# The q part of a 5x5 grouped convolution on TensorE: fp32 products replaced by three products of split fp32r operands

## Chip, cores and metric

One Trainium2 chip, one of its cores. The metric is the device time of one execution, in microseconds; lower is better. The median of three executions of the kernel before is 5199.48 us (5190.54 to 5200.01).

## The reference, cut to what matters

Two layers on 4 images of 512 channels, 64x64 pixels. The change lies in the first one, a multi-scale linear attention:

```python
q = h @ wq.T; k = h @ wk.T; v = h @ wv.T                       # 512x512 each
qkv = moveaxis(concatenate([q, k, v], -1), -1, 1)
dw = conv(qkv, dw_kernel, 5x5, 'SAME', one group per channel)
pw = conv(dw, pw_kernel, 1x1, groups of 8 channels)
qkv_all = concatenate([qkv, pw], axis=1)
f = qkv_all.reshape(B, -1, 3 * 8, N)
query, key_ = relu(f[:, :, :8]), relu(f[:, :, 8:16]); value = f[:, :, 16:]
scores = einsum('bhdn,bhen->bhde', value_and_ones, key_)
out = einsum('bhde,bhen->bhdn', scores, query)
out = out[:, :, :-1] / (out[:, :, -1:] + 1e-15)
y = batchnorm(conv1x1(out)) + x
```

The second layer (edge filters, GELU, a gate, a 1x1 convolution and a layer norm) is not touched.

## The kernel before

The first layer runs in 16 passes: 4 images by 4 sets of 16 groups of channels ("heads"). A pass has two stages.

The *plain* stage computes q, k and v of the pass in 8 chunks of 512 pixels. It already uses split operands: ScalarE rounds x into `x_hi` (type fp32r), VectorE and GpSimd compute `x_lo` = x - x_hi, and TensorE adds three products, `w_hi x_hi`, `w_lo x_hi` and `w_hi x_lo` (lines 356 to 358). The results go to DRAM as tiles of 4x4 pixels with a halo, and come back as `loaded`, one head at a time, four buffers deep. At the end of the stage `mask_scores` writes the sums of the keys into `score_d` (lines 589 and 591) and TensorE multiplies `relu_q` by it (`denominate`, line 398); VectorE then inverts the sums (`invert`, line 628).

The *convolution* stage runs over 16 heads h. The depthwise 5x5 and pointwise 1x1 kernels of a head are multiplied into one matrix per shift of the tile grid: GpSimd's `build` makes `toeplitz` with three multiplications of 128x512 (t = q, k, v; line 733), two buffers deep, and starts on head h when TensorE has ended head h-2. TensorE's `conv_head` does q first: 4 matrix products of 128x128 by 256 columns in fp32 (line 431), each of which shows as two records, then k and v: 2 x 8 products of 128 columns each (line 441), two records each, with data that ScalarE's `gather` has laid out as `columns`. ScalarE copies q and v out of PSUM, VectorE k (`ckey_t`, line 671).

Order on the engines of the convolution stage, which is the order in the code:

- ScalarE, head h: gather(h+1), q out of PSUM (line 545), v of head h out of PSUM (line 485, the helper `copy`).
- VectorE, head h: `ckey_t` of head h; for h = 4 to 11 `divide`, two multiplications of 128x256 that wait for a load of `inverse`; at h = 3 `mixed_weights`; at h = 7 `split_weights` for the next pass, a cast of 128x1536 to `w_hi` and a subtraction to `w_lo` (lines 605 and 607), in 15 of the 16 passes.
- GpSimd: `build` for heads 2 to 15. Those for heads 0 and 1 lie in the plain stage.
- SyncE issues all DMAs: the q results to DRAM, the load of a later head, and the writes and loads of `divide`.

Of the kernel before, what the change touches and what calls it, by code (L numbers as in the profile page):

```python
# [6 lines left out]
F32 = mybir.dt.float32  # L7
# [3 lines left out]
F32R = mybir.dt.float32r  # L11
# [4 lines left out]
P = 128  # L16
# [38 lines left out]
def attention(nc, banks, io, dram):  # L55

    with ExitStack() as ctx:
        def sb(name, shape):
            return ctx.enter_context(nc.sbuf_tensor(name, shape, F32))
# [21 lines left out]
        value_t = sb("value_t", [P, 2, 4, P + 1])  # L81
        ckey_t = sb("ckey_t", [P, HV * PL, P])
        cvalue_t = sb("cvalue_t", [P, HV * PL, P + 1])
        loaded = sb("loaded", [P, LR, 3, TN])
        columns = sb("columns", [P, 2, 2, HV + 1, TG * HT])
        toeplitz = sb("toeplitz", [P, 2, 3, len(SHIFTS) * M])
        q_stage = sb("q_stage", [M, 2, TT])
        score_n = sb("score_n", [P, P])
        score_d = sb("score_d", [P, NCH * P])
        score_t = sb("score_t", [P, P])  # L90
        w_proj = sb("w_proj_part", [P, C])
        scale_row = sb("scale_row", [P, C])
# [48 lines left out]
        columns_ready = sem("columns_ready")  # L141
        head_done = sem("head_done")
        toeplitz_ready = sem("toeplitz_ready")
        cready = [sem(f"conv_{n}_ready") for n in "qk"]
        cevac = [sem(f"conv_{n}_evacuated") for n in "qkv"]
        q_written = [sem(f"q_written{i}") for i in range(2)]
# [39 lines left out]
        with nc.Block() as block:  # L186
# [161 lines left out]
            def _(pe):  # L348
# [41 lines left out]
                def denominate(it, half):  # L390
                    pe.wait_ge(sums_placed, 2 * it + half + 1)
                    if half == 0:
                        pe.wait_ge(evac[T_Q], NCH * (it + 1))
                    else:
                        pe.wait_ge(conv_q_loaded, 16 * (it + 1))
                    pe.wait_ge(den_evac, START + 2 * it + half)
                    for j in range(NCH):
                        last = nc.tensor.matmul(DEN_BANK[:, :], score_d[:, j * P:(j + 1) * P], rows((relu_q, relu_c)[half], j),
                                                start=(j == 0), stop=(j == NCH - 1))
                    last.then_inc(summed, 1)  # L400

# [20 lines left out]
                def conv_head(it, h):  # L422
                    w = toeplitz[:, h % 2, :, :].rearrange("p t (d m) -> p t d m", m=M)
                    q_bank, k_bank, v_bank = (of[h % 2] for of in CONV_BANKS)
                    x_q = loaded[:, h % LR, T_Q, :].rearrange("p (a c) -> p a c", c=TG)
                    pe.wait_ge(tiles_loaded[h % LR], 16 * (SH // LR) * it + 16 * (h // LR) + 16)
                    pe.wait_ge(toeplitz_ready, SH * it + h + 1)
                    if h >= 2:
                        pe.wait_ge(cevac[T_Q], SH * it + h - 1)
                    for d, (a, b) in enumerate(SHIFTS):  # L430
                        last = nc.tensor.matmul(q_bank[0:M, 0:TT], w[:, T_Q, d, :], x_q[:, a:a + TO, b:b + TO],  # L431
                                                start=(d == 0), stop=(d == len(SHIFTS) - 1))
                    last.then_inc(cready[T_Q], 1)

                    pe.wait_ge(columns_ready, SH * it + h + 1)
                    for t, bank in ((T_K, k_bank), (T_V, v_bank)):
                        if h >= 2:
                            pe.wait_ge(cevac[t], SH * it + h - 1)
                        for v in range(HV):
                            for d, (a, b) in enumerate(SHIFTS):  # L440
                                last = nc.tensor.matmul(bank[:, v * M:(v + 1) * M],  # L441
                                                        columns[:, h % 2, t - T_K, v + b, a * HT:(a + TO) * HT],
                                                        w[:, t, d, :], start=(d == 0), stop=(d == len(SHIFTS) - 1))
                        last.then_inc(cready[T_K] if t == T_K else head_done, 1)
# [38 lines left out]
            def _(act):  # L483
# [28 lines left out]
                def plain(it, conv_of):  # L512
                    if conv_of is not None:
                        act.wait_ge(divided, START + at(conv_of, 1, 0))
                    for j in range(NCH):
                        if j >= 2:
                            value_by_position(it, j - 2)
                        if conv_of is not None:
                            if j == 2:
                                scores_to_mix(conv_of, 1)  # L520
                        query(it, j)
                        if j + 1 < NCH:
                            round_x(it, j + 1)
                        key(it, j)
                    value_by_position(it, NCH - 2)
                    value_by_position(it, NCH - 1)

                def gather(it, h):

# [6 lines left out]
                    last.then_inc(columns_ready, 1)  # L536

                def conv(it, last):
                    gather(it, 0)
                    for h in range(SH):  # L540
                        if h + 1 < SH:
                            gather(it, h + 1)
                        act.wait_ge(cready[T_Q], SH * it + h + 1)
                        act.wait_ge(q_written[h % 2], 16 * START + 16 * (SH // 2 * it + h // 2))
                        nc.scalar.activation(q_stage[:, h % 2, :], CONV_BANKS[T_Q][h % 2][0:M, 0:TT], ACT.Relu).then_inc(cevac[T_Q], 1)
                        if h == 1:
                            scores_to_mix(it, 0)
                        if not last and h == SH - 2:
                            round_x(it + 1, 0)
                        act.wait_ge(head_done, SH * it + h + 1)  # L550
                        to = cvalue_t[:, :, h * HD:(h + 1) * HD].rearrange("p (s r) o -> p s r o", s=HV)
                        copy(to, CONV_BANKS[T_V][h % 2][:, 0:HV * M].rearrange("p (s o r) -> p s r o", o=HD, r=PL)).then_inc(cevac[T_V], 1)
# [19 lines left out]
            def _(dve):  # L572
# [6 lines left out]
                def mask_scores(it, half):  # L579

                    if half:
                        dve.wait_ge(scores_ready, it + 1)
                    else:
                        dve.wait_ge(chunk_scored, NCH * (it + 1))
                    nc.vector.tensor_copy(key_sum[:, :], SCORE_BANK[:, P:P + 1]).then_inc(key_sum_ready, 1)
                    dve.wait_ge(key_sum_ready, 2 * it + half + 1)
                    dve.wait_ge(den_evac, START + 2 * it + half)
                    apart, last = P + SH, (NCH - 1) * (P + SH)
                    nc.vector.tensor_scalar(score_d[:, 0:last].rearrange("p (j s) -> p j s", s=apart)[:, :, 0:SH],
                                            mask[:, None, :].to_broadcast([P, NCH - 1, SH]), key_sum[:, 0:1], None, ALU.mult)  # L590
                    nc.vector.tensor_scalar(score_d[:, last:last + SH], mask[:, :], key_sum[:, 0:1], None,
                                            ALU.mult).then_inc(sums_placed, 1)
                    dve.wait_ge(score_turned, 2 * it + half)
                    nc.vector.tensor_tensor(score_n[:, :].rearrange("p (h d) -> p h d", d=HD),
                                            SCORE_BANK[:, 0:P].rearrange("p (h d) -> p h d", d=HD),
                                            mask[:, :, None].to_broadcast([P, SH, HD]), ALU.mult).then_inc(scores_masked, 1)
# [44 lines left out]
                def mixed_weights(it, half):  # L641
                    dve.wait_ge(bn_inverted, 2)
                    dve.wait_ge(w_mixed, 2 * it + half + 1)
                    nc.vector.tensor_tensor(w_proj[:, :], W_BANKS[half][:, :], scale_row[:, :], ALU.mult).then_inc(w_out_ready, 1)

                def plain(it, conv_of):
                    for j in range(NCH):
                        if j == 4 and conv_of is not None:
# [10 lines left out]
                            split_x(it, j + 1)  # L659
                        value(it, j)  # L660
                        compress(it, j)
                    keys_by_position(it, NCH - 2)
                    keys_by_position(it, NCH - 1)
                    mask_scores(it, 0)
                    invert(it, 0)

                def conv(it, more):
                    for h in range(SH):
                        dve.wait_ge(cready[T_K], SH * it + h + 1)
                        to = ckey_t[:, :, h * HD:(h + 1) * HD].rearrange("p (s r) o -> p s r o", s=HV)  # L670
                        nc.vector.tensor_scalar(  # L671
# [45 lines left out]
            def _(pool):  # L717
# [5 lines left out]
                def build(it, h):  # L723
# [4 lines left out]
                    for t in range(3):  # L728
# [3 lines left out]
                        point = g[:, NTAP:GT][:, None, :, None].to_broadcast([P, len(SHIFTS), HD, PL])  # L732
                        last = nc.gpsimd.tensor_tensor(  # L733
                            toeplitz[:, h % 2, t, :].rearrange("p (d o r) -> p d o r", o=HD, r=PL), tap, point, ALU.mult)
                    last.then_inc(toeplitz_ready, 1)

                def plain(it):
# [695 lines left out]
```

## Time and profile before

| | |
|---|---|
| median of three executions | 5199.48 us |
| the profiled execution | 5196.7 us |
| its span, first to last instruction | 5194.8 us |
| mean clock of TensorE granted, as a share of full speed | 0.976 |
| TensorE, matrix products busy | 4887.5 us, 94% |
| VectorE busy | 2583.4 us, 50% |
| ScalarE busy | 2021.1 us, 39% |
| GpSimd busy | 1223.1 us, 24% |
| lines 356 to 358, the split products of the plain stage | 1536 each, 610.9, 599.7 and 601.2 us |
| line 431, q of the convolution | 2048 records, 485.9 us |
| line 441, k and v of the convolution | 8192 records, 955.7 us |

PE is TensorE, PEld its loads of weights, DVE VectorE, ACT ScalarE, POOL GpSimd. Records of TensorE overlap, as matrix products are pipelined: the distance from one start to the next tells what one costs, not its duration. The first layer takes up the first 3114 us or so of the span, the second layer the rest.

### The profile page before, as it was taken

The page shows a single profiled execution, that of the slowest core. Times are in us where ns is not written, and L with a number is a line of the kernel's source. Part 1 is how long each engine was busy: PE and PEld are TensorE (multiplying, and loading weights), DVE is VectorE, ACT ScalarE, POOL GpSimd, SP SyncE. Part 2 cuts the span into 40 slices and gives each one's busy share as a digit, 9 for nine tenths or more (in the row PEclk, how much of TensorE's full clock was granted, in tenths as well). Part 3 has the DMA queues.
Part 4 walks back from the last instruction along what each step waited for, and adds up shares of the span by engine and source line. Part 5 has one row for each costly group of instructions (what it writes and reads, how often), then busy time and mean ns, then how long its engine had stood idle before and what let it go on. Part 6 is the DMA issues. An engine that isn't in the chain of part 4 may idle for free. (4 is left out here: it accounts for less than half of the span.)

```text
span 5194.8 us, 65292 instructions
## 1 busy us (share of the span) xinstructions
PE 4887.5 (94%) x22760; PEld 3445.3 (66%) x22760; DVE 2583.4 (50%) x3635; ACT 2021.1 (39%) x3671; POOL 1223.1 (24%) x1030
## 2 busy tenths in 40 slices
PE   8999999999999999999999996899899989998958
PEld 7887887888888888888888883344344434443423
DVE  3333333333334334424434421786688578847865
ACT  3333333333333333333323320454555455545555
POOL 2342342342342332332332330000300020011003
PEclk9999999999999999999999998999999999999969
DMA  6666665666666666666656644443344344434313
GB/s 188 198 208 202 197 214 199 198 212 205 198 216 202 204 206 206 206 197 215 206 186 225 203 151 168 142 155 112 130 136 150 108 144 130 141 118 135 117 35 115
DMA packets 390811, 893.09 MB, mean 172 GB/s; under 512 B 33488, under 2 KB 66512, under 8 KB 388240
## 3 DMA queue, kind: packets, MB, share of 16 engines
q1 hardware_dynamic: 390544, 889.18, 51.8%
q8 instruction: 211, 3.46, 0.3%
q14 instruction: 56, 0.46, 0.0%
HBM read 588.74 MB, written 300.32 MB: 171 GB/s over the span
## 5 line engine op out<-in xcount | busy, mean ns | idle before, releaser
L733 POOL TENSOR_TENSOR toeplitz<-taps 128x512 f32<-128x512 f32 x768 | 889.1, 1185 | 955.2 <-PE bank L441 955.2
L441 PEld LDWEIGHTS bank<-toeplitz,columns 128*128 128x128 f32 x8192 | 954.4, 192 | 13.9
L441 PE MATMUL bank<-toeplitz,columns 128*128 128x128 f32 x8192 | 955.7, 275 | 0.0
L1029 PE MATMUL bank<-att,w_proj 128*128 128x512 f32 x2048 | 909.6, 598 | 34.1 <-DVE centred L1314 23.8
L1029 PEld LDWEIGHTS bank<-att,w_proj 128*128 128x128 f32 x2048 | 393.0, 192 | 531.8 <-issue 523.3
L356 PE MATMUL bank<-x_hi,w_hi 128*128 128x512 f32 x1536 | 610.9, 398 | 18.4 <-DVE x_lo L600 18.4
L1362 POOL TENSOR_TENSOR centred<-centred,x_out 128x512 f32<-128x512 f32 x128 | 164.5, 1318 | 1937.1 <-ACT centred L1176 1937.1
L358 PE MATMUL bank<-x_lo,w_hi 128*128 128x512 f32 x1536 | 601.2, 391 | 0.0
L357 PE MATMUL bank<-x_hi,w_lo 128*128 128x512 f32 x1536 | 599.7, 390 | 0.0
L1042 PE MATMUL bank<-edge,w_branch 128*128 128x512 f32 x1024 | 494.5, 629 | 96.1 <-ACT edge L1130 96.1
L671 DVE TENSOR_SCALAR ckey_t<-bank 128x256 f32<-128x256 f32 x256 | 107.4, 419 | 881.8 <-PE bank L441 881.4
L431 PE MATMUL bank<-loaded,toeplitz 128*128 128x256 f32 x2048 | 485.9, 379 | 3.4 <-POOL toeplitz L733 3.4
L1064 PE MATMUL bank<-feat,w_image 128*128 128x512 f32 x1024 | 453.4, 601 | 10.3 <-DVE w_image L1330 10.3
L600 DVE TENSOR_TENSOR x_lo<-x_sb,x_hi 128x1536 fp32r<-128x1536 f32 x128 | 251.7, 1966 | 421.9 <-ACT x_hi L485 421.9
L1042 PEld LDWEIGHTS bank<-edge,w_branch 128*128 128x128 f32 x1024 | 204.1, 202 | 370.8 <-issue 283.4
L720 POOL TENSOR_TENSOR x_lo<-x_sb,x_hi 128x512 fp32r<-128x512 f32 x128 | 165.6, 1293 | 1074.5 <-ACT x_hi L485 1074.5
L431 PEld LDWEIGHTS bank<-loaded,toeplitz 128*128 128x128 f32 x2048 | 370.5, 190 | 62.0 <-issue 15.5
L485 ACT ACTIVATE cvalue_t<-bank 128x256 f32<-128x256 f32 x256 | 102.6, 401 | 773.7 <-PE bank L441 773.7
L1064 PEld LDWEIGHTS bank<-feat,w_image 128*128 128x128 f32 x1024 | 197.0, 193 | 259.2 <-issue 249.8
L356 PEld LDWEIGHTS bank<-x_hi,w_hi 128*128 128x128 f32 x1536 | 289.6, 189 | 76.3 <-DMA mask<-in_head_mask 12.6
L358 PEld LDWEIGHTS bank<-x_lo,w_hi 128*128 128x128 f32 x1536 | 289.4, 188 | 62.3
L357 PEld LDWEIGHTS bank<-x_hi,w_lo 128*128 128x128 f32 x1536 | 289.9, 189 | 57.6
(115 smaller groups left out, 5629.8 us busy)
## 6 DMA issues: line engine op xcount, KB each, us to landing
x_sb<-in_x_tiled SPq DMA_DIRECT2D x128, 1024.0 KB, 6.4
tiles_dram<-tiles SPq DMA_DIRECT2D x128, 867.0 KB, 6.8
loaded<-tiles_dram SPq DMA_DIRECT2D x256, 433.5 KB, 4.0
inverse<-inverse_dram SPq DMA_DIRECT2D x256, 256.0 KB, 5.0
att_dram<-out_sb SPq DMA_DIRECT2D x256, 256.0 KB, 4.1
att<-att_dram SPq DMA_DIRECT2D x64, 1024.0 KB, 6.3
xb<-x_dram SPq DMA_DIRECT2D x128, 330.0 KB, 3.2
x_out<-in_x_pad SPq DMA_DIRECT2D x32, 1056.0 KB, 5.5
```

Of the source, the lines that this page charges most:

```text
L356: nc.tensor.matmul(banks[t][:, :], wh, xh, start=(k == 0), stop=False)
L357: nc.tensor.matmul(banks[t][:, :], wl, xh, start=False, stop=False)
L358: last = nc.tensor.matmul(banks[t][:, :], wh, xl, start=False, stop=(k == KT - 1))
L431: last = nc.tensor.matmul(q_bank[0:M, 0:TT], w[:, T_Q, d, :], x_q[:, a:a + TO, b:b + TO], start=(d == 0), stop=(d == len(SHIFTS) - 1))
L441: last = nc.tensor.matmul(bank[:, v * M:(v + 1) * M], columns[:, h % 2, t - T_K, v + b, a * HT:(a + TO) * HT], w[:, t, d, :], start=(d == ...
L600: nc.vector.tensor_tensor(x_lo[:, j % XR, X_DVE, :], x_sb[:, j % XR, X_DVE, :], x_hi[:, j % XR, X_DVE, :].bitcast(F32), ALU.subtract).then ...
L720: nc.gpsimd.tensor_tensor(x_lo[:, j % XR, X_POOL, :], x_sb[:, j % XR, X_POOL, :], x_hi[:, j % XR, X_POOL, :].bitcast(F32), ALU.subtract).t ...
L733: last = nc.gpsimd.tensor_tensor(toeplitz[:, h % 2, t, :].rearrange("p (d o r) -> p d o r", o=HD, r=PL), tap, point, ALU.mult)
L1029: last = nc.tensor.matmul(P_BANKS[m][:, :], w_proj[:, i * HALF + k, m * P:(m + 1) * P], att[:, i, k, :], start=(i == 0 and k == 0), stop=( ...
L1042: last = nc.tensor.matmul(banks[e][:, :], w_branch[:, k, e, :], edge[:, k % 2, e, :], start=(k == 0), stop=(k == KT - 1))
L1064: last = nc.tensor.matmul(Z_BANKS[n % len(Z_BANKS)][:, :], w_image[:, k, m * P:(m + 1) * P], feat[:, k, j * CH:(j + 1) * CH], start=(k == ...
L1362: nc.gpsimd.tensor_tensor(y, y, x_out[:, j % 2, m, :].rearrange("p (r w) -> p r w", w=W2)[:, :, 1:W + 1], ALU.add).then_inc(out_ready, 1)
```

## The change

The q part of the convolution takes split operands too.

- ScalarE rounds q's tiles of a head into `q_hi` (`round_q`, 128x289) and q's matrices into `tq_hi` (`round_taps`, 128x512). Both have one buffer. In head h it does this for head h+1, right after q has been copied out of PSUM, ahead of the copy of v.
- VectorE subtracts: `split_q` (128x289) and `split_taps` (128x512), for head h+1, at the top of head h, ahead of `ckey_t`. The differences `q_lo` and `tq_lo` take the places of `loaded` and `toeplitz` in memory.
- TensorE does 12 products of 256 columns in fp32r in place of 4 in fp32. They wait for `q_split` and `tq_split`; the wait for all three matrices of a head moves behind q.
- For head 0, `round_taps` lies in the plain stage on ScalarE at j = 5, `split_taps` on VectorE at j = 6, `round_q` at the head of the convolution stage and `split_q` between `mask_scores` and `invert`.
- `score_d` shrinks from 1024 to 240 columns. One write of 128x16 takes the place of writes of 128x112 and 128x16, and TensorE reads it at 8 offsets.

```diff
@@ -81,12 +81,18 @@
...
         cvalue_t = sb("cvalue_t", [P, HV * PL, P + 1])
-        loaded = sb("loaded", [P, LR, 3, TN])
+        with nc.sbuf_tensor("loaded", [P, LR, 3, TN], F32) as loaded:
+            pass
+        q_lo = ctx.enter_context(nc.sbuf_tensor("q_lo", [P, LR, 3, TN], F32R))
         columns = sb("columns", [P, 2, 2, HV + 1, TG * HT])
-        toeplitz = sb("toeplitz", [P, 2, 3, len(SHIFTS) * M])
+        with nc.sbuf_tensor("toeplitz", [P, 2, 3, len(SHIFTS) * M], F32) as toeplitz:
+            pass
+        tq_lo = ctx.enter_context(nc.sbuf_tensor("tq_lo", [P, 2, 3, len(SHIFTS) * M], F32R))
+        tq_hi = ctx.enter_context(nc.sbuf_tensor("tq_hi", [P, len(SHIFTS) * M], F32R))
+        q_hi = ctx.enter_context(nc.sbuf_tensor("q_hi", [P, TN], F32R))
         q_stage = sb("q_stage", [M, 2, TT])
         score_n = sb("score_n", [P, P])
-        score_d = sb("score_d", [P, NCH * P])
+        score_d = sb("score_d", [P, 2 * P - SH])
         score_t = sb("score_t", [P, P])
@@ -395,7 +406,7 @@
...
                     for j in range(NCH):
-                        last = nc.tensor.matmul(DEN_BANK[:, :], score_d[:, j * P:(j + 1) * P], rows((relu_q, relu_c)[half], j),
+                        last = nc.tensor.matmul(DEN_BANK[:, :], score_d[:, P - SH * (j + 1):2 * P - SH * (j + 1)], rows((relu_q, relu_c)[half], j),
                                                 start=(j == 0), stop=(j == NCH - 1))
@@ -422,16 +433,22 @@
...
                     q_bank, k_bank, v_bank = (of[h % 2] for of in CONV_BANKS)
-                    x_q = loaded[:, h % LR, T_Q, :].rearrange("p (a c) -> p a c", c=TG)
-                    pe.wait_ge(tiles_loaded[h % LR], 16 * (SH // LR) * it + 16 * (h // LR) + 16)
-                    pe.wait_ge(toeplitz_ready, SH * it + h + 1)
+                    wide = tq_hi[:, :].rearrange("p (d m) -> p d m", m=M)
+                    x_hi_q = q_hi[:, :].rearrange("p (a c) -> p a c", c=TG)
+                    x_lo_q = q_lo[:, h % LR, T_Q, :].rearrange("p (a c) -> p a c", c=TG)
+                    pe.wait_ge(q_split, SH * it + h + 1)
+                    pe.wait_ge(tq_split, SH * it + h + 1)
                     if h >= 2:
...
                     for d, (a, b) in enumerate(SHIFTS):
-                        last = nc.tensor.matmul(q_bank[0:M, 0:TT], w[:, T_Q, d, :], x_q[:, a:a + TO, b:b + TO],
-                                                start=(d == 0), stop=(d == len(SHIFTS) - 1))
+                        high, low = x_hi_q[:, a:a + TO, b:b + TO], x_lo_q[:, a:a + TO, b:b + TO]
+                        narrow = tq_lo[:, h % 2, T_Q, d * M:(d + 1) * M]
+                        nc.tensor.matmul(q_bank[0:M, 0:TT], wide[:, d, :], high, start=(d == 0), stop=False)
+                        nc.tensor.matmul(q_bank[0:M, 0:TT], narrow, high, start=False, stop=False)
+                        last = nc.tensor.matmul(q_bank[0:M, 0:TT], wide[:, d, :], low, start=False, stop=(d == len(SHIFTS) - 1))
                     last.then_inc(cready[T_Q], 1)
+                    pe.wait_ge(toeplitz_ready, SH * it + h + 1)
                     pe.wait_ge(columns_ready, SH * it + h + 1)
@@ -521,9 +538,19 @@
...
                             round_x(it, j + 1)
+                        if j == 5:
+                            round_taps(it, 0)
                         key(it, j)
...
                     value_by_position(it, NCH - 1)
+
+                def round_q(it, h):
+                    act.wait_ge(tiles_loaded[h % LR], 16 * (SH // LR) * it + 16 * (h // LR) + 16)
+                    copy(q_hi[:, :], loaded[:, h % LR, T_Q, :]).then_inc(q_rounded, 1)
+
+                def round_taps(it, h):
+                    act.wait_ge(tq_built, SH * it + h + 1)
+                    copy(tq_hi[:, :], toeplitz[:, h % 2, T_Q, :]).then_inc(tq_rounded, 1)
@@ -536,6 +563,7 @@
...
                 def conv(it, last):
+                    round_q(it, 0)
                     gather(it, 0)
@@ -543,6 +571,9 @@
...
                         nc.scalar.activation(q_stage[:, h % 2, :], CONV_BANKS[T_Q][h % 2][0:M, 0:TT], ACT.Relu).then_inc(cevac[T_Q], 1)
+                        if h + 1 < SH:
+                            round_q(it, h + 1)
+                            round_taps(it, h + 1)
                         if h == 1:
@@ -585,10 +616,7 @@
...
                     dve.wait_ge(den_evac, START + 2 * it + half)
-                    apart, last = P + SH, (NCH - 1) * (P + SH)
-                    nc.vector.tensor_scalar(score_d[:, 0:last].rearrange("p (j s) -> p j s", s=apart)[:, :, 0:SH],
-                                            mask[:, None, :].to_broadcast([P, NCH - 1, SH]), key_sum[:, 0:1], None, ALU.mult)
-                    nc.vector.tensor_scalar(score_d[:, last:last + SH], mask[:, :], key_sum[:, 0:1], None,
+                    nc.vector.tensor_scalar(score_d[:, P - SH:P], mask[:, :], key_sum[:, 0:1], None,
                                             ALU.mult).then_inc(sums_placed, 1)
@@ -642,6 +670,14 @@
...
                     nc.vector.tensor_tensor(w_proj[:, :], W_BANKS[half][:, :], scale_row[:, :], ALU.mult).then_inc(w_out_ready, 1)
+
+                def split_q(it, h):
+                    dve.wait_ge(q_rounded, SH * it + h + 1)
+                    nc.vector.tensor_tensor(q_lo[:, h % LR, T_Q, :], loaded[:, h % LR, T_Q, :], q_hi[:, :].bitcast(F32), ALU.subtract).then_inc(q_split, 1)
+
+                def split_taps(it, h):
+                    dve.wait_ge(tq_rounded, SH * it + h + 1)
+                    nc.vector.tensor_tensor(tq_lo[:, h % 2, T_Q, :], toeplitz[:, h % 2, T_Q, :], tq_hi[:, :].bitcast(F32), ALU.subtract).then_inc(tq_split, 1)
@@ -659,13 +695,19 @@
...
                         compress(it, j)
+                        if j == 6:
+                            split_taps(it, 0)
                     keys_by_position(it, NCH - 2)
...
                     mask_scores(it, 0)
+                    split_q(it, 0)
                     invert(it, 0)
...
                     for h in range(SH):
+                        if h + 1 < SH:
+                            split_q(it, h + 1)
+                            split_taps(it, h + 1)
                         dve.wait_ge(cready[T_K], SH * it + h + 1)
@@ -732,6 +774,8 @@
...
                             toeplitz[:, h % 2, t, :].rearrange("p (d o r) -> p d o r", o=HD, r=PL), tap, point, ALU.mult)
+                        if t == T_Q:
+                            last.then_inc(tq_built, 1)
                     last.then_inc(toeplitz_ready, 1)
```

Left out of the diff are the five new semaphores.

## Rows read from the trace of the kernel before

**Rows 1.** The page: busy time of TensorE, its busy tenths and clock
```profile
PE 4887.5 (94%) x22760; PEld 3445.3 (66%) x22760; DVE 2583.4 (50%) x3635; ACT 2021.1 (39%) x3671; POOL 1223.1 (24%) x1030
...
PE   8999999999999999999999996899899989998958
...
PEclk9999999999999999999999998999999999999969
```

**Rows 2.** One convolution stage: busy PE, PEld, DVE, ACT, POOL, then clock
```profile
1467.00:1555.00 88.00, 87.33 (x654) 82.98 (x653) 29.04 (x38) 29.40 (x77) 47.30 (x43) 1.00 0.63 200
```

**Rows 3.** Waits of TensorE, 300 to 3100 us: us in total, times, longest
```profile
PE bank L398 <- DVE score_d L591: 13.7, 14, 1.0
...
PE bank L431 <- POOL toeplitz L733: 3.2, 9, 0.5
```

**Rows 4.** Timeline, head 7 of one pass: start, duration, engine, operation
```profile
1505.43 1.90 PE L431 MATMUL bank<-loaded,toeplitz 128*128 128x256 f32 x8
...
1505.67 3.34 POOL L733 TENSOR_TENSOR toeplitz<-taps 128x512 f32<-128x512 f32 x3 [2.22 <-PE bank L441]
1505.91 1.17 ACT L485 ACTIVATE columns<-loaded 128x272 f32<-128x272 f32 x3
...
1507.16 3.73 PE L441 MATMUL bank<-toeplitz,columns 128*128 128x128 f32 x32
1507.36 0.38 ACT L545 ACTIVATE q_stage<-bank 128x256 f32<-128x256 f32 x1 [0.27 <-PE bank L431]
...
1509.34 0.41 DVE L671 TENSOR_SCALAR ckey_t<-bank 128x256 f32<-128x256 f32 x1
...
1510.73 1.89 PE L431 MATMUL bank<-loaded,toeplitz 128*128 128x256 f32 x8
```

**Rows 5.** The same timeline, VectorE and GpSimd in heads 8 and 9
```profile
1510.96 1.90 DVE L637 TENSOR_TENSOR out_sb<-relu_q,inverse 128x256 f32<-128x256 f32 x2 [1.22 <-DMA inverse<-inverse_dram]
1510.97 4.39 POOL L733 TENSOR_TENSOR toeplitz<-taps 128x512 f32<-128x512 f32 x3 [1.97 <-PE bank L441]
...
1512.70 1.76 DVE L605 CAST w_hi<-w_sb 128x1536 fp32r<-128x1536 f32 x1
...
1514.49 2.49 DVE L607 TENSOR_TENSOR w_lo<-w_sb,w_hi 128x1536 fp32r<-128x1536 f32 x1
...
1516.28 4.17 POOL L733 TENSOR_TENSOR toeplitz<-taps 128x512 f32<-128x512 f32 x3 [0.91 <-PE bank L441]
```

**Rows 6.** Timeline of TensorE, split products of 512 columns in the plain stage
```profile
1587.07 0.39 PE L357 MATMUL bank<-x_hi,w_lo 128*128 128x512 f32 x1
1587.30 0.39 PE L358 MATMUL bank<-x_lo,w_hi 128*128 128x512 f32 x1
```

**Rows 7.** Instructions by source line, 300 to 3100 us: duration ns min/median/max
```profile
L600 DVE TENSOR_TENSOR x_lo<-x_sb,x_hi x112: 1748/1759/2604, 390.2 to 2982.7; 128x1536 fp32r<-128x1536 f32 x112
...
L605 DVE CAST w_hi<-w_sb x14: 946/1762/1773, 350.8 to 2860.9; 128x1536 fp32r<-128x1536 f32 x14
...
L485 ACT ACTIVATE x_hi<-x_sb x224: 621/1050/1487, 383.1 to 2981.2; 128x512 fp32r<-128x512 f32 x112
```

**Rows 8.** Timeline, end of a plain stage and first head
```profile
1459.73 0.28 DVE L589 TENSOR_SCALAR score_d<-mask,key_sum 128x112 f32<-128x112 f32 x1
1459.93 0.22 DVE L591 TENSOR_SCALAR score_d<-mask,key_sum 128x16 f32<-128x16 f32 x1
...
1468.38 3.35 DVE L628 RECIPROCAL den_sb<-den_sb 128x512 f32<-128x512 f32 x1
```

**Rows 9.** A wait of TensorE, then three stretches (columns of Rows 2)
```profile
4955.88 7.62 PE L1042 MATMUL bank<-edge,w_branch 128*128 128x512 f32 x11 [4.02 <-ACT edge L1130]
...
4946.00:4951.00 5.00, 4.53 (x7) 1.98 (x8) 4.45 (x7) 2.60 (x5) 0.00 (x0) 0.66 0.26 68
...
4955.00:4961.00 6.00, 5.12 (x6) 2.19 (x7) 5.83 (x10) 4.14 (x7) 0.00 (x0) 0.50 0.21 56
...
1454.00:1462.00 8.00, 4.81 (x28) 3.63 (x29) 2.82 (x8) 3.10 (x8) 0.00 (x0) 1.00 0.80 289
```

More of the change, by code:

```diff
@@ L143, in attention @@
         toeplitz_ready = sem("toeplitz_ready")
+        tq_built = sem("toeplitz_q_built")
+        tq_rounded = sem("toeplitz_q_rounded")
+        tq_split = sem("toeplitz_q_split")
+        q_rounded = sem("q_tiles_rounded")
+        q_split = sem("q_tiles_split")
         cready = [sem(f"conv_{n}_ready") for n in "qk"]
```

## The prediction

> **What bounds the kernel now.** I read the page first. TensorE is busy 94% of the span, and in the first 24 of the 40 slices, the first layer, its digit is 9 after one 8, and so is the clock's in nearly all [rows 1]. Next, the busy time of one convolution stage: 87.33 of 88 us on TensorE, every other engine at most 54% [rows 2]. Then what TensorE waits for between 300 and 3100 us: in the convolution stage only 3.2 us, for GpSimd's matrices [rows 3]. So in this stage time is made of TensorE's cadence, and last the timeline gives that cadence. In head 7, q starts at 1505.43, k and v at 1507.16, the next q at 1510.73 [rows 4]. Head: 5.30 us; q 1.73, k and v 3.57. Shorten q and the head gets shorter, as long as what feeds q is ready in time. That is what the change puts at stake: q now waits for a chain over two engines with single buffers.
>
> **The products.** Removed per head: 1.73 us. Added: 12 products of 256 columns in fp32r. No row shows that width. From above: split products of 512 columns start 0.227 us apart [rows 6], where two fp32 streams of 256 columns, with their loads, take 1.73/8 = 0.217. If the extra 0.010 to 0.014 us is a fixed cost of each fp32r product, one of 256 columns costs 0.107 + 0.014 = 0.121. From below: line 441 loads a 128x128 matrix for every record and starts one each 3.57/32 = 0.112 us; nothing in the stage does better. I take the middle, 0.117, so 12 x 0.117 = 1.40 us, 0.33 less per head, 256 x 0.33 = **84 us saved** (with 0.112: 100; with 0.121: 72). The head becomes 4.97 us.
>
> The Trainium skill (TensorE: Matmul & The Clock Gate, Back-to-back issue gap) gives 262 cycles for 256 columns, 0.109 us; by that the sum would save 24 us more than mine. It states this without naming fp32r, and the fp32r rows at 512 columns lie above its rule (518 cycles, 0.216 us), so the row decides.
>
> **The chain for the next q, in a usual head.** Count from q's start in head h. ScalarE gathers head h+1 until 1.65 (1507.08 - 1505.43) [rows 4]. q's last product ends near 1.6. Then q out of PSUM, 0.38; `round_q` of 289 columns, about 0.45 (gather's 272 take 1.17/3 = 0.39 each); `round_taps` of 512, 0.63 (the 621 ns minimum) [rows 4, 7]. Adjacent ones overlap by 0.1, so `q_hi` is there at 2.4 and `tq_hi` at 3.0. VectorE subtracts: line 600 takes 1.75 for 1536 columns with two SBUF inputs [rows 7], so 1.04 ns a column plus 0.15: 0.45 for `split_q`, 0.68 for `split_taps`. GpSimd builds until 0.24 + 3.08 = 3.3, and holds VectorE up: see below. `split_q` 3.3 to 3.6, `split_taps` to 4.3. q of h+1 may start at 4.3; TensorE is free at 4.97. The chain hides with 0.7 us to spare, and k and v of head h are its cover. Without it, q would wait in each of 256 heads. `ckey_t`, now behind the splits, ends near 4.6 instead of 4.3; k's bank is wanted two heads later. v's copy waits for v anyway. ScalarE's load, 0.3+1.17+0.38+1.1 = 3.0 of 4.97, fits.
>
> **The turns at the port.** The rows show that VectorE's subtractions and multiplications with two SBUF inputs, and its cast, don't run beside GpSimd's multiplications; one waits for the other. Line 605 takes 0.946 at least and 1.76 in the middle [rows 7]; here 1.76, while three builds take 4.39 us in place of 3.08 (line 600 alone shows that 2.49 for `w_lo` is 0.74 too much) [rows 5, 7]. They take strict turns, since each engine's next instruction asks after its last has let go. Per turn: a build 0.95, a half of `divide` 0.35, `w_hi` 0.85, `w_lo` 1.65, and from these widths `split_q` 0.35, `split_taps` 0.65.
>
> In heads 4 to 11 `divide` delays the builds by up to two turns, 0.7 us, and so the splits. At worst I get the last split at 4.9 after q's start: still under 4.97.
>
> **Heads 7 to 9, where it doesn't fit.** `split_weights` stands in head 7 of VectorE, ahead of the splits for head 9. Count from q's start in head 8. `divide` starts near 0.05, behind the splits for head 8. Turns: half 0.35, build 0.95, half 0.35, build 0.95, `w_hi` 0.85, build 0.95, `w_lo` 1.65: over at 6.1. (Before, it ended at 1516.98 - 1510.73 = 6.25 in this pass [rows 4, 5], harmless, since TensorE needed nothing from it.) Meanwhile head 8 has ended at 4.97, and GpSimd asks for its turn with the build for head 10. So: build 0.95, `split_q` 0.35, build 0.95, `split_taps` 0.65 and 0.1 to be seen: q of head 9 starts at 9.1 to 9.2 and not at 4.97. **4.2 us lost in each of 15 passes, 63 us.** Late next is only `ckey_t` of head 8, behind the splits, and `divide`, whose loads of `inverse` SyncE sends; splits for head 10 find GpSimd done. Bounds: 2.3 us if GpSimd gets no turn in between (34 us), 4.6 with a late `inverse` (69).
>
> **What that wait does to the clock.** In the last stage TensorE waits 4.02 us for `edge` again and again; right after, the clock stands at 0.50 for a stretch with 5.12 us of work, and at 0.66 in one of 5 us after another such wait [rows 9]: that is 1.2 in place of 2.4 GHz, 2.6 and 1.7 us lost. A stretch at the end of a plain stage with 3.2 idle us of 8, in pieces, leaves it at 1.00 [rows 9]. TensorE would idle about 4 us here, after and before dense work. I take 2.0 us per pass, **30 us**; bounds 0 and 2.6 x 15 = 39.
>
> **The rest.** In head 0 the inversion (3.35 us from 1468.38) [rows 8] ends 4.4 after q's start; the splits for head 1 follow it and end at 5.3, TensorE is free at 4.97 + 0.11: 0.2 x 16 = 3 us lost. The smaller `score_d` takes 0.20 us off (line 591 starts that much after 589) [rows 8], and TensorE waits for it [rows 3]: 16 x 0.2 = 3 us saved. The waits for GpSimd at q, 3.2 us by the record and some 5 with what the modelled ends hide [rows 3], go: the wait for the whole build is behind q now. `round_taps` and `split_taps` of the plain stage, 0.6 and 0.7 us once a pass, lie beside chunks of about 10 us of products; below that cover, they would cost 21 us. The steps for head 0 at the head of the convolution stage lie under `denominate`, 7 us. SyncE's order and the number of DMAs don't change.
>
> **Sum.** -84 - 5 - 3 + 3 + 63 + 30 = +4 us. The profiled execution took 5196.7 (span 5194.8 and 1.9 around it), 2.8 below the median; on the median, 5199.5 + 4 = 5203.
>
> **Rivals.** (1) The turns and the wait are as above, but the clock stays up: no row shows a lone wait of 4 us in dense work of this stage. Sum -26: 5173. Against it: each wait of 4.02 us in the last stage looks alike. (2) GpSimd gets no turn between the splits; TensorE idles 2.3 us, and the clock loses 10 us at most: -84 - 5 + 34 + 10 = -45, 5154. Against it: the turns in rows 5. (3) Slower by more: the chain doesn't fit in the usual head. It decides from 0.7 us: with a longer semaphore path or one more build turn between `split_q` and `split_taps`, the last split lands at 5.2 to 5.3, 0.3 x 240 = 72 us more: 5275. For it: `build` is already pushed back in 8 of the heads. (4) fp32r products of 256 columns read from rows of 16 don't stream at one column per cycle. At the fp32 rate of 0.217 x 2 each, 12 take 5.2 us, 3.5 more than before: 5199 + 890 = 6090. Against it: 512 columns run at 0.227. (5) The products take 0.112, all else as forecast: 5188.
>
> **How the numbers follow.** A measurement of this kernel can tell about 0.2%, 10 us, from no change. My forecast, 5190 to 5232 with the bounds of product and clock: 0.45; of that, faster 0.05, same 0.25, slower 0.15. Rival 1: 0.18, rival 2: 0.12, rival 5: 0.10, all nearly faster. Rival 3: 0.11, rival 4: 0.04, slower. Together faster 0.42, same 0.28, slower 0.30. The range 5145 to 5240 leaves out rivals 4, most of 3, and a little at the lower end. Forecast's own range: 5180 to 5230.
>
> **What would show it.** In the timeline after: q's first record to k's first, 1.34 to 1.45 us. Usual heads 4.9 to 5.0 apart. TensorE's wait for VectorE's `tq_lo` ahead of head 9 near 4 us, 15 times, and none over 0.3 elsewhere; around it the turns build, `split_q`, build, `split_taps`. A dip of the clock's digits between slices 1 and 24. Wrong, if heads 2 to 7 are longer than 5.1, if `split_taps` follows `split_q` at once behind `w_lo`, or if the clock stays up.

## The result

The changed kernel takes 5218.09 us (median of 6 runs, 5216.56 to 5224.15), the kernel before 5197.91 (median of 6): the ratio is 1.0043, 95% interval 1.0031 to 1.0056, so 0.43% slower, some 20 us. The forecast was 5203, within 5145 to 5240, and gave slower a chance of 0.30. The profiled execution is the slowest of the six, 5224.15 us, with a span of 5222.3. The medians and ratios of the experiments leave out two executions at a lower granted clock: 13090.41 us (0.507) of the second experiment and 5833.38 us (0.835) of the fourth.

The page after: TensorE's busy share is 93%, its tenths look as before [rows 1], and so do the clock's. I had expected a dip in the clock's digits, and there is none: a slice is 130 us long, and a wait of 4 us in it, with the slow microseconds behind it, doesn't change a digit. The mean over the whole span shows it, 0.969 against 0.976.

```profile
PE 4858.9 (93%) x23784; PEld 3468.8 (66%) x23784; DVE 2946.3 (56%) x4115; ACT 2236.4 (43%) x4183; POOL 1222.0 (23%) x1030
...
PE   8999999999999999999999996899899989998958
...
PEclk9999999999999999999999998999999999999969
```

The waits of TensorE between 300 and 3100 us, which is where it shows (us in total, times, longest): 15 waits, 3.5 us each, ahead of q's first product. "issue" means that the record names no releaser. The waits for GpSimd's matrices at q [rows 3] are gone, and the one for `score_d` is 2.6 us shorter.

```profile
PE bank L446 <- issue: 52.8, 15, 3.9
...
PE bank L409 <- DVE score_d L619: 11.1, 14, 0.8
```

A usual head after, the timeline of head 6 in the same pass as [rows 4]. Read it as a chain. q's products start every 0.125 us (eleven steps from 1511.89 to k's first at 1513.27; the stamp of the group's first product is early by some 0.1 us, and behind products of 512 columns, which end head 1, by 0.4). q leaves PSUM at 1513.56, `q_hi` and `tq_hi` follow, `split_q` waits for the last build (1.13 us in place of 0.45), `split_taps` ends at 1516.04, and TensorE starts the next q at 1516.76, right behind v: 5.08 us after the last.

```profile
1511.68 0.37 PE L446 MATMUL bank<-q_hi,tq_hi 128*128 128x256 f32 x1
...
1511.89 0.29 PE L447 MATMUL bank<-q_hi,tq_lo 128*128 128x256 f32 x1
...
1512.01 3.10 POOL L775 TENSOR_TENSOR toeplitz<-taps 128x512 f32<-128x512 f32 x3 [1.97 <-PE bank L458]
...
1513.14 0.29 PE L448 MATMUL bank<-q_lo,tq_hi 128*128 128x256 f32 x1
...
1513.27 3.73 PE L458 MATMUL bank<-toeplitz,columns 128*128 128x128 f32 x32
1513.56 0.38 ACT L573 ACTIVATE q_stage<-bank 128x256 f32<-128x256 f32 x1
1513.84 0.44 ACT L502 ACTIVATE q_hi<-loaded 128x289 fp32r<-128x289 f32 x1
...
1514.17 0.62 ACT L502 ACTIVATE tq_hi<-toeplitz 128x512 fp32r<-128x512 f32 x1
1514.31 1.13 DVE L676 TENSOR_TENSOR q_lo<-loaded,q_hi 128x289 fp32r<-128x289 f32 x1 [2.01 <-ACT q_hi L502]
...
1515.36 0.68 DVE L680 TENSOR_TENSOR tq_lo<-toeplitz,tq_hi 128x512 fp32r<-128x512 f32 x1
...
1515.96 0.41 DVE L713 TENSOR_SCALAR ckey_t<-bank 128x256 f32<-128x256 f32 x1
...
1516.76 0.37 PE L446 MATMUL bank<-q_hi,tq_hi 128*128 128x256 f32 x1
```

Heads 8 and 9, the answer to [rows 5]. `w_lo` ends at 1528.38, 6.3 us after q's start. Then the turns: a build, `split_q` until 1529.61, a build, `split_taps` until 1531.06. q of head 9 starts at 1531.17 after an idle 3.74 us; the head took 9.05 us.

```profile
1522.12 0.36 PE L446 MATMUL bank<-q_hi,tq_hi 128*128 128x256 f32 x1
1522.16 3.61 POOL L775 TENSOR_TENSOR toeplitz<-taps 128x512 f32<-128x512 f32 x3 [1.99 <-PE bank L458]
...
1522.62 2.37 DVE L665 TENSOR_TENSOR out_sb<-relu_q,inverse 128x256 f32<-128x256 f32 x2 [0.27 <-DMA inverse<-inverse_dram]
...
1523.69 3.74 PE L458 MATMUL bank<-toeplitz,columns 128*128 128x128 f32 x32
...
1524.83 1.76 DVE L633 CAST w_hi<-w_sb 128x1536 fp32r<-128x1536 f32 x1
...
1526.62 1.76 DVE L635 TENSOR_TENSOR w_lo<-w_sb,w_hi 128x1536 fp32r<-128x1536 f32 x1
...
1527.51 4.47 POOL L775 TENSOR_TENSOR toeplitz<-taps 128x512 f32<-128x512 f32 x3 [1.74 <-PE bank L458]
...
1528.30 1.31 DVE L676 TENSOR_TENSOR q_lo<-loaded,q_hi 128x289 fp32r<-128x289 f32 x1
1529.53 1.53 DVE L680 TENSOR_TENSOR tq_lo<-toeplitz,tq_hi 128x512 fp32r<-128x512 f32 x1
...
1531.17 0.55 PE L446 MATMUL bank<-q_hi,tq_hi 128*128 128x256 f32 x1 [3.74 <-issue]
```

The clock over the same microseconds (columns of [rows 2], the clock is third from the end): 1.00 before the wait, 0.50 right after it.

```profile
1522.00:1527.00 5.00, 4.96 (x43) 4.91 (x43) 4.69 (x6) 2.69 (x7) 3.61 (x3) 1.00 0.68 216
1527.00:1531.00 4.00, 0.43 (x4) 0.24 (x3) 4.00 (x4) 1.44 (x4) 3.49 (x3) 1.00 1.00 323
1531.00:1534.00 3.00, 2.83 (x13) 2.87 (x14) 1.95 (x4) 0.00 (x0) 0.98 (x1) 0.50 0.11 40
```

### The profile page after: what moved, and what is told of

Its sections match the earlier page's. It is cut to its first block and busy times, and to the rows that moved or that the text cites. A ratio compares the mean times of both kernels' runs of the same rounds, so it can differ in the third digit from the quotient of the medians.

```text
span 5222.3 us, 68364 instructions
## 1 busy us (share of the span) xinstructions
PE 4858.9 (93%) x23784; PEld 3468.8 (66%) x23784; DVE 2946.3 (56%) x4115; ACT 2236.4 (43%) x4183; POOL 1222.0 (23%) x1030
## 5 line engine op out<-in xcount | busy, mean ns | idle before, releaser
L458 PE MATMUL bank<-toeplitz,columns 128*128 128x128 f32 x8192 | 967.5, 277 | 0.0
L676 DVE TENSOR_TENSOR q_lo<-loaded,q_hi 128x289 fp32r<-128x289 f32 x256 | 236.0, 922 | 490.7 <-ACT q_hi L502 490.6
L446 PE MATMUL bank<-q_hi,tq_hi 128*128 128x256 f32 x1024 | 332.0, 324 | 58.0 <-issue 56.4
L448 PE MATMUL bank<-q_lo,tq_hi 128*128 128x256 f32 x1024 | 301.4, 294 | 0.0
```

The lines of the kernel that those rows point to most:

```text
L446: nc.tensor.matmul(q_bank[0:M, 0:TT], wide[:, d, :], high, start=(d == 0), stop=False)
L448: last = nc.tensor.matmul(q_bank[0:M, 0:TT], wide[:, d, :], low, start=False, stop=(d == len(SHIFTS) - 1))
L458: last = nc.tensor.matmul(bank[:, v * M:(v + 1) * M], columns[:, h % 2, t - T_K, v + b, a * HT:(a + TO) * HT], w[:, t, d, :], start=(d == ...
L676: nc.vector.tensor_tensor(q_lo[:, h % LR, T_Q, :], loaded[:, h % LR, T_Q, :], q_hi[:, :].bitcast(F32), ALU.subtract).then_inc(q_split, 1)
```

## The experiments

Each was run beside the kernel before on the same chip, the first four on one chip, the others on a second: its ratio is to the kernel before there. The median spacing of the heads comes from the starts of q's first products in each trace, over the 16 passes.

**The weights' split in heads 12 and 13.** Is VectorE's backlog at `split_weights` the cause?

```diff
-                        if more and h == 7:
+                        if more and h == 12:
+                            round_weights(it + 1)
+                        if more and h == 13:
                             split_weights(it + 1)
```

(`round_weights` is the cast with its load's wait, `split_weights` the subtraction.)

> The changed kernel, with the cast to w_hi moved from head 7 to head 12 of VectorE and the subtraction to w_lo to head 13, where divide is over. Theory (backlog on VectorE): the wait of 3.74 us ahead of head 9's q goes, heads 8 and 9 take 5.07 us like the others in place of 9.0 and 6.4 to 7.6, and no half-clock stretch is left in the convolution stage. That is 15 x (3.95 + 1.3 or more) = 80 us less: about 5138 us. Rival (VectorE has too little room in any head, so the wait only moves): the same wait ahead of head 14 or 15, within 15 us of the changed kernel's 5218.

5137.79 us, ratio 0.9889 (0.9874 to 0.9904). Head 8 has a median of 5.07 us, head 9 of 5.06; head 14 takes 5.20. In its timeline `w_lo` of head 13 runs until 1131.57 and pushes the build to 1134.73, the build pushes both splits, and `split_taps` ends at 1135.28, 0.1 us before q starts. That is 0.13 us in each of 15 passes, 2 us. The long wait is gone and next to nothing came back for it: the rival falls. One wait is left in the profiled run, in head 7 of one pass. The timeline shows whose it is: `divide` waited 4.97 us for its load of `inverse` and kept the splits behind it on VectorE. Behind this wait too the clock is down, 0.64 over the 4 us from 1483. So a late load can do what the weights did, but once in 16 passes, not in 15.

```profile
1476.09 3.74 PE L458 MATMUL bank<-toeplitz,columns 128*128 128x128 f32 x32
...
1479.09 1.09 DVE L667 TENSOR_TENSOR out_sb<-relu_q,inverse 128x256 f32<-128x256 f32 x2 [4.97 <-DMA inverse<-inverse_dram]
...
1482.84 0.36 PE L446 MATMUL bank<-q_hi,tq_hi 128*128 128x256 f32 x1 [3.01 <-issue]
```

**Work inside the wait.** Is head 9 long because of the clock?

```diff
+                    if h == 9:
+                        pe.wait_ge(den_evac, START + 2 * it + 1)
+                        for j in range(4):
+                            nc.tensor.matmul(DEN_BANK[:, :], ident[:, :], rows(relu_q, j), start=True, stop=True)
                     pe.wait_ge(q_split, SH * it + h + 1)
```

> The changed kernel; in head 9, ahead of the wait for the splits, TensorE does 4 extra fp32 products of 512 columns into the idle bank of the denominators (3.4 us of work whose result nobody reads). The wait stays, but TensorE isn't idle in it. Theory (the 1.3 to 2.5 us too much in head 9 are the clock at half): head 8 stays at 9.0 us, head 9 falls to 5.07, 15 x 1.4 = 21 us less, about 5197. Rival (head 9 is long because its own inputs are late): no change, 5218.

5198.84 us, ratio 1.0012 (1.0003 to 1.0022), 0.31% below the changed kernel's. Head 8 keeps its 8.97 us, head 9 falls from 6.53 to 5.05. The extra products fill the wait up to 0.21 us, and the stretch behind it is at full clock, where the changed kernel's was at 0.50. Useless work saved 16 us. It would be more if it were left out of the last pass, which has no wait there: the same products cost 3.4 us in it. The inputs of head 9 come as late as before, so the rival falls.

```profile
1510.40 3.60 PE L442 MATMUL bank<-relu_q,ident 128*128 128x512 f32 x8
1514.22 0.36 PE L450 MATMUL bank<-q_hi,tq_hi 128*128 128x256 f32 x1 [0.21 <-issue]
...
1514.00:1519.00 5.00, 4.79 (x42) 4.82 (x42) 4.18 (x9) 1.24 (x3) 1.03 (x1) 1.00 0.44 110
```

**No build turns.** Are two of GpSimd's turns part of the wait?

```diff
                         pool.wait_ge(head_done, SH * it + h - 1)
+                    if h == 10:
+                        pool.wait_ge(tq_split, SH * it + h)
                     for t in range(3):
```

> The changed kernel; GpSimd's build for head 10 starts only when the splits for head 9 are done, so that no build turn lies between w_lo and the two splits. split_weights stays in head 7. Theory (two build turns of 0.95 us are part of the wait): head 8 takes 9.0 - 1.9 = 7.1 us, TensorE idles under 2 us there, and the clock falls less often: 29 us less from the wait, 5 to 20 from the clock, 5170 to 5185. Rival (the port isn't it, the splits are late by VectorE's own work alone): head 8 stays at 9.0, 5218.

5178.92 us, ratio 0.9965 (0.9954 to 0.9977). Head 8 takes 7.27 us. The two splits now follow `w_lo` back to back, 0.45 and 0.68 us, and the build starts behind them:

```profile
1498.18 2.49 DVE L635 TENSOR_TENSOR w_lo<-w_sb,w_hi 128x1536 fp32r<-128x1536 f32 x1
...
1500.60 0.45 DVE L676 TENSOR_TENSOR q_lo<-loaded,q_hi 128x289 fp32r<-128x289 f32 x1
1500.97 0.68 DVE L680 TENSOR_TENSOR tq_lo<-toeplitz,tq_hi 128x512 fp32r<-128x512 f32 x1
...
1501.73 3.60 POOL L777 TENSOR_TENSOR toeplitz<-taps 128x512 f32<-128x512 f32 x3 [2.67 <-DVE tq_lo L680]
1501.75 0.36 PE L446 MATMUL bank<-q_hi,tq_hi 128*128 128x256 f32 x1 [1.93 <-DVE q_lo L676]
```

So the wait of 3.7 us was 1.8 us of turns and 1.9 us of the weights' split itself. Head 9 took 5.06 us in 9 of the 15 passes and 6.6 in the other 6: about 2 us of idling drops the clock sometimes, 3.7 us dropped it in each of the 15.

**fp32 products in the chain.** Do the products set a usual head? Rounding and splitting stay, the low parts are left out of the products.

```diff
-                        nc.tensor.matmul(q_bank[0:M, 0:TT], wide[:, d, :], high, start=(d == 0), stop=False)
-                        nc.tensor.matmul(q_bank[0:M, 0:TT], narrow, high, start=False, stop=False)
-                        last = nc.tensor.matmul(q_bank[0:M, 0:TT], wide[:, d, :], low, start=False, stop=(d == len(SHIFTS) - 1))
+                        last = nc.tensor.matmul(q_bank[0:M, 0:TT], wide[:, d, :].bitcast(F32), high.bitcast(F32), start=(d == 0), stop=(d == len(SHIFTS) - 1))
```

> The changed kernel with all rounding and splitting kept, but q's convolution is done by 4 fp32 products of the high parts (the low parts are left out of the computation). Theory (usual heads are set by TensorE's products, 5.30 against 5.07 us): usual heads go back to 5.30, head 8 stays near 9.0 as it is tied to VectorE, so about 225 x 0.235 = 53 us more, about 5271. Rival (the chain over ScalarE and VectorE sets the 5.07 us): heads of 5.07 to 5.1, 5218.

5247.31 us (median of three), ratio 1.0096 (1.0078 to 1.0115). Usual heads are back at 5.30 us. That is weaker than I had written: with TensorE's own work at 5.30 us, a chain that takes 5.07 would leave 5.30 as well, so this run doesn't decide against the rival. What decides is the 0.7 us that head 6 has to spare, and the run with 256 columns in a row below: there the chain is the same, only the products are shorter, and the head gets shorter with them. The kernel came out 28 us above the changed one by the ratios, where 53 were expected. Head 8 takes 9.25 to 9.45 us in 7 of the 15 passes but 7.75 in the other 8, and heads 8 and 9 together take 13 us less than in the changed kernel. In one of the 8 passes, the first half of `divide` came before the build asked for its turn, and `w_lo` ended 4.9 us after q's start in place of 6.6. So the turns fall differently here; I had taken them as fixed.

**256 columns in a row, and 288.** Both on top of the weights' move, both with a q that isn't the convolution's. The first replaces the operands as shown; the second has 288 in place of 256, in the products' output too.

```diff
                         high, low = x_hi_q[:, a:a + TO, b:b + TO], x_lo_q[:, a:a + TO, b:b + TO]
                         narrow = tq_lo[:, h % 2, T_Q, d * M:(d + 1) * M]
+                        high, low = q_hi[:, 0:256], q_lo[:, h % LR, T_Q, 0:256]
```

> The kernel with the weights' split in heads 12 and 13, with q's moving operand read as 256 columns in a row in place of 16 rows of 16 out of 17 (so the convolution's q is another sum, the work the same in size). q's products now start 0.124 us apart. If the short rows are what puts them above the 0.117 that was forecast, they come down to 0.112 to 0.118 and a usual head to 4.9 to 5.0 us. Rival (a fixed cost of each fp32r product, whatever the layout): 0.124 stays, heads of 5.07.

> As the contiguous one, with 288 columns per product. If a product costs its columns at 2.4 GHz and a fixed 0.017 us, they start 0.120 + 0.017 = 0.137 us apart and q takes 1.65 us. If the cost is a share of the width (0.124 is 16% over 0.107), 0.139; if it is bound by the load of weights and not by columns, it stays at 0.124.

One execution each: 5129.17 us (median head 5.00) and 5151.88 us (5.17). In the timeline of the first, eleven steps from 1509.23 to 1510.53 make 0.118 us per product:

```profile
1509.23 0.28 PE L448 MATMUL bank<-q_hi,tq_lo 128*128 128x256 f32 x1
...
1510.42 0.28 PE L449 MATMUL bank<-q_lo,tq_hi 128*128 128x256 f32 x1
1510.53 1.72 PE L459 MATMUL bank<-toeplitz,columns 128*128 128x128 f32 x14
```

of the second, eleven from 1506.46 to 1507.91 make 0.132:

```profile
1506.46 0.29 PE L448 MATMUL bank<-q_hi,tq_lo 128*128 128x288 f32 x1
...
1507.91 1.27 PE L459 MATMUL bank<-toeplitz,columns 128*128 128x128 f32 x10
```

Over 176 heads of each trace (3 to 7 and 10 to 15 of every pass) the mean steps are 0.119 and 0.133, and 0.125 in the changed kernel. 32 more columns cost 0.014 us, and 32 at 2.4 GHz are 0.0133. So a product costs its columns and a fixed 0.012 us (0.119 - 256/2400; at 512 columns [rows 6] it is 0.227 - 0.213 = 0.014). The short rows, 16 of 17, cost another 0.006 us a product. The run also changed the column at which three of the four shifts start, but not that of the first, whose products take 0.123 and 0.125 with short rows and 0.118 and 0.120 without: so it is the rows. Both counted, the layout and a fixed cost, and the loads of weights did not set the pace.

**The same move without split products.** The kernel before with the edit of the first experiment.

> The kernel before the change, with the same move of the weights' cast and subtraction to heads 12 and 13. Tells what the move is worth without split products. Theory (TensorE waits there only for GpSimd's builds, 0.3 to 0.7 us in 10 of 15 passes): 5 us less, ratio 0.999. Rival (the 80 us that the move gave the changed kernel have little to do with the change's chain): some 50 us or more less here too.

5186.80 us, ratio 0.9986 (0.9976 to 0.9995). All heads of the convolution from 2 on take 5.30 us, 5 us less over head 8 by the trace. So the move is worth little by itself, and the changed kernel's 80 us were its own conflict with `split_weights`. With the move in both, split products bring 1% (0.9889 against 0.9986).

**The inversion behind the splits for head 1.** On top of the weights' move too.

```diff
                     split_q(it, 0)
-                    invert(it, 0)
...
                             split_taps(it, h + 1)
+                        if h == 0:
+                            invert(it, 0)
```

> The changed kernel with the weights' split in heads 12 and 13, and the inversion of the sums (4 us on VectorE) behind the splits for head 1 in place of ahead of them. Theory: head 0 loses 0.34 us in each of 16 passes to the inversion, so 5 us less than with the weights' move alone, ratio to before 0.988. Rival (the inversion is then late for divide or the splits for head 2, which cost the same or more): ratio 0.989 or above.

5131.91 us, ratio 0.9883 (0.9866 to 0.9899). Head 0 falls from a median of 5.84 to 5.50 us, and heads 1 to 6 stay. Here the splits for head 1 come first, and the 3.35 us of the inversion lie beside v and the next q:

```profile
1434.60 0.46 DVE L678 TENSOR_TENSOR q_lo<-loaded,q_hi 128x289 fp32r<-128x289 f32 x1 [9.16 <-ACT q_hi L502]
...
1435.11 0.69 DVE L682 TENSOR_TENSOR tq_lo<-toeplitz,tq_hi 128x512 fp32r<-128x512 f32 x1
1435.72 0.68 DVE L656 TENSOR_SCALAR den_sb<-bank 128x512 f32<-128x512 f32 x1
1436.44 3.35 DVE L658 RECIPROCAL den_sb<-den_sb 128x512 f32<-128x512 f32 x1
...
1437.15 0.37 PE L446 MATMUL bank<-q_hi,tq_hi 128*128 128x256 f32 x1
```

The 5.4 us (16 x 0.34) are clear in the trace; the two ratios' intervals overlap, so the timing alone doesn't tell this kernel from the first experiment's. By its median it is the fastest version tried that computes the convolution, 1.2% below the kernel before and 1.6% below the changed one.

## Why the forecast held, and where it was off

**The products: right in kind, mis-sized.** Forecast 0.117 us each, 1.40 us a q and 84 us in all; measured 0.125, 5.07 us a head in place of 4.97, 256 x 0.23 = 60 us. From q's first record to k's it is 1.59 us, where I had said 1.34 to 1.45. This term is off by 24 us, more than the whole error of the sum. I had 0.121 as the upper bound, from the surplus at 512 columns alone. That bound left out the layout: q's rows of 16 out of 17 cost 0.006 more, and the contiguous run gave 0.119, inside my bounds. The fp32 q had read the same rows at 0.217 us a record [rows 4], and twice 256 columns at 2.4 GHz are 0.213, so no surcharge was visible; that misled me. By the Trainium skill (TensorE: Matmul & The Clock Gate, Back-to-back issue gap) 256 columns take 262 cycles, 0.109 us; the measurement, 0.119 at best, decides against it for fp32r.

**The chain in a usual head: right.** Forecast: last split at 4.3 us after q's start, 0.7 to spare. Measured in head 6: 1516.04 - 1511.68 = 4.36, and 0.7 to spare. q_hi and tq_hi came at 2.6 and 3.1 (forecast 2.4 and 3.0). Heads 3 to 6 have a median of 5.07 and no wait. That products, not the chain, set this was shown by the shorter products of the contiguous run: same chain, 5.00 us. Rival 3 falls. I had named heads 2 to 7 over 5.1 us as a sign of being wrong. Head 2 reads 5.39, but only by the early stamp behind 512 columns; from k's first product to the next head's it takes 5.07. Head 7 does break the limit, with 5.18 (up to 5.6): some 3 us in all, where `divide` pushes the splits. I had put it just inside.

**Heads 8 and 9: right.** Forecast: `w_lo` over at 6.1, q of head 9 at 9.1 to 9.2, 63 us lost. Measured: 6.3, 9.05, and by the starts over 15 passes 51 us more in head 8 than before; with the 4 us that q saves there and the 5 us of waits for GpSimd that went, 60 us. That `split_weights` is the cause was shown by moving it; that two build turns were 1.8 us of it, by holding the build back. Rival 2 falls. The Trainium skill (SBUF — State Buffer, Who interferes with whom) has it that a VectorE instruction with two SBUF inputs and a GpSimd one that reads SBUF exclude each other for a whole instruction; the trace agrees, `split_q` takes 1.31 us behind a build and 0.45 alone.

**The clock: right, a little less than forecast.** 30 us forecast, 24 measured: head 9 took 19.7 us more than before over the passes and should have taken 4.5 less. That it is the clock was shown by filling the wait. Rival 1 falls: in dense work too, a lone wait of 3.7 us brings 1.2 GHz behind it. [Rows 9], from another stage, gave the price: 1.7 and 2.6 us a wait, 1.6 here.

**The rest.** The inversion costs 0.34 us in head 0, not 0.2, as VectorE's `split_q` can't start until 1484.36:

```profile
1481.09 3.35 DVE L656 RECIPROCAL den_sb<-den_sb 128x512 f32<-128x512 f32 x1
...
1481.55 3.74 PE L458 MATMUL bank<-toeplitz,columns 128*128 128x128 f32 x32
...
1484.36 0.40 DVE L676 TENSOR_TENSOR q_lo<-loaded,q_hi 128x289 fp32r<-128x289 f32 x1
1484.67 0.68 DVE L680 TENSOR_TENSOR tq_lo<-toeplitz,tq_hi 128x512 fp32r<-128x512 f32 x1
...
1485.50 0.36 PE L446 MATMUL bank<-q_hi,tq_hi 128*128 128x256 f32 x1
```

`score_d` is as forecast (2.6 us less waiting in 14 passes). The wait for builds at q went, as forecast.

**The sum again, with what was measured:** -60 products - 5 waits for builds - 3 `score_d` + 5 inversion + 60 wait at head 9 + 24 clock + 3 heads 7 = +24 us, and the medians differ by 20. The terms are read from the two profiled executions, which are 27 us apart; the rest lies outside the heads. Forecast was +4; the term of the products explains 24 of the difference, wait and clock give 9 back, and inversion and head 7 take 5. That two errors of opposite sign met, +24 and -9 us, is luck, and the 15 us left were enough to miss the direction: my chances had faster first (0.42), and slower, which it is, at 0.30. Rival 5 (0.112) and rival 4 (no full rate) fall by the measured 0.125.

Open: why short rows cost more in fp32r and not in fp32. Only one layout against one other was tried, in one execution.

## What to carry to other kernels

When an operand gets a preparing step on another engine with one buffer, don't ask only whether the step is short against the period. Walk that engine's list for the longest thing that can stand in front of it once a pass: here 4 us of weight splitting that nobody had ever waited for turned a gain of 60 us into a loss of 20, and moving it to heads where the engine is free gave 1.1% instead. Price each such wait with what the clock takes after it; if a wait of several microseconds can't be avoided, work without use in it may pay.

## What the runs showed of the hardware that I had not expected

- An fp32r product of 256 columns costs its columns at 2.4 GHz and 0.012 us when they lie in a row (0.119; 288 columns 0.133), and 0.125 in rows of 16 out of 17. fp32 at the same rows takes 0.217 a record, two of them a product, without a visible surcharge.
- 3.4 us of products whose result nobody reads, put into an idle of 3.7 us, made the kernel 16 us faster.
- Which of VectorE and GpSimd gets the next turn can hang on little: with 0.23 us more per head, head 8 took 7.75 us in 8 passes and 9.25 to 9.45 in 7, where the changed kernel took 8.95 to 9.26 in all 15.
